# A four-layer transformer stack on one core: other order at the ends of the attentions, and transposes ahead of the first work

## The reference

```python
# L0: self-attention, cross-attention, MLP
x = x + attention(LN(x) @ w_qkv, mask=ltor) @ w_ao        # 16 heads of 16
x = x + attention(LN(x) @ w_q, enc @ w_kv, mask=cross) @ w_co
x = x + gelu_tanh(LN(x) @ w1 + b1) @ w2 + b2              # inner width 1024
# L1: RWKV block: token shift, a recurrence over 64 steps, a gated feed-forward
# L2: two cross-attentions of 16 heads of 128, then an MLP with exact gelu
# L3: cross-attention with 16 heads of 16, then an MLP with tanh gelu
```

## Time and profile before

| | us |
|---|---|
| median of 3 runs | 2081.22 |
| lowest and highest | 2080.62, 2081.76 |
| the profiled execution | 2083.29 |
| its span | 2081.5 |
| TensorE busy | 1927.9 (93%) |
| VectorE, ScalarE, GpSimd busy | 1220.0, 1049.1, 1038.6 |

### The profile page before, as it was taken

The page is one execution under the profiler, slowest core; times in us unless marked ns, Lnnn a source line. Parts: engine busy times, 40 slices in busy tenths (PEclk is TensorE's granted clock), DMA queues, the critical chain, the costliest instruction groups (busy, mean ns, idle before and its releaser), DMA issues.

```text
span 2081.5 us, 39329 instructions
## 1 busy us (share of the span) xinstructions
PE 1927.9 (93%) x15072; PEld 1567.9 (75%) x15072; DVE 1220.0 (59%) x2136; ACT 1049.1 (50%) x1949; POOL 1038.6 (50%) x1132
## 2 busy tenths in 40 slices
PE   6999799988785679999999999999999999999799
PEld 4777689433443559899989989898998988967688
DVE  3566646388999555555555555555555556745555
ACT  3665543323242356656566565656656565345542
POOL 5777731376574165445454544545444454346620
PEclk9999899989898899999999999999999999999899
DMA  4010010000000013332323332232333320010000
GB/s 183 2 42 2 2 53 1 1 0 1 1 1 31 21 44 90 90 90 86 91 79 90 89 90 90 81 95 81 90 89 88 91 67 21 21 41 2 2 11 31
DMA packets 61848, 108.08 MB, mean 52 GB/s; under 512 B 7008, under 2 KB 42336, under 8 KB 60256
## 3 DMA queue, kind: packets, MB, share of 16 engines
q1 hardware_dynamic: 60784, 103.34, 16.3%
q10 hardware_dynamic: 880, 2.22, 0.3%
HBM read 103.44 MB, written 2.10 MB: 51 GB/s over the span
## 4 chain that ended last, share of the span: by engine, by line
PE 61%; DVE 3%; issue 2%; ACT 1%; POOL 1%; DVEq 0%; ACTq 0%; POOLq 0%
PE banks L791 18%; PE banks L820 9%; PE banks L863 9%; PE banks L852 5%; PE banks L589 4%; PE banks L606 4%; PE banks L833 4%; PE banks L841 1%; PE banks L440 1%; PE banks L431 1%; PE banks L417 1%; PE banks L513 1%; PE banks L488 1%; PE banks L773 1%; ACT xn L919 1%
## 5 line engine op out<-in xcount | busy, mean ns | idle before, releaser
L1866 POOL TENSOR_TENSOR w_lo<-w2ring,w_hi 128x512 fp32r<-128x512 f32 x128 | 166.2, 1298 | 293.5 <-ACT w_hi L1187 293.5
L1246 ACT ACTIVATE PT<-banks 64x256 f32<-64x256 f32 x256 | 96.6, 377 | 264.7 <-PE banks L841 261.6
L1631 DVE SCALAR_TENSOR_TENSOR c_lo<-banks,cols,c_hi 128x512 fp32r<-128x512 f32 x128 | 96.1, 751 | 201.1 <-ACT c_hi L1211 201.1
L1875 POOL TENSOR_TENSOR wo_lo<-wo_ring,wo_hi 128x256 fp32r<-128x256 f32 x128 | 94.2, 736 | 173.3 <-ACT wo_hi L1217 173.3
L863 PE MATMUL banks<-wo_hi,c_hi 128*128 128x256 f32 x512 | 150.2, 293 | 1.8 <-POOL wo_lo L1875 1.8
L863 PE MATMUL banks<-wo_hi,c_lo 128*128 128x256 f32 x512 | 145.1, 283 | 0.0
L863 PE MATMUL banks<-wo_lo,c_hi 128*128 128x256 f32 x512 | 145.0, 283 | 0.0
L852 PEld LDWEIGHTS banks<-PT,v 128*128 128x128 f32 x1024 | 133.6, 192 | 9.0 <-ACT PT L1246 0.4
L852 PE MATMUL banks<-PT,v 128*128 128x128 f32 x1024 | 135.8, 276 | 0.3 <-ACT PT L1246 0.3
L1204 ACT ACTIVATE k<-banks,cols 128x512 f32<-128x512 f32 x128 | 88.0, 687 | 86.7 <-PE banks L791 86.7
L431 PE MATMUL banks<-xm,wl 128*128 128x512 f32 (+2 forms) x208 | 114.9, 700 | 16.1 <-DVE xm L1471 7.7
(11 more groups left out here) (219 smaller groups left out, 5773.3 us busy)
## 6 DMA issues: line engine op xcount, KB each, us to landing
w2ring<-in_w SPq DMA_DIRECT2D x128, 384.0 KB, 3.0
b2ring<-in_b SPq DMA_DIRECT2D x128, 128.0 KB, 3.3
wo_ring<-in_wo SPq DMA_DIRECT2D x128, 128.0 KB, 2.2
mlp_w<-in_mlp SPq DMA_DIRECT2D x6, 1024.0 KB, 5.4
wl<-in_wres SPq DMA_DIRECT2D x1, 2656.0 KB, 8.8
X<-in_x_in SPq DMA_DIRECT2D x4, 512.0 KB, 11.5
ctx_tok<-in_ctx_in SPq DMA_DIRECT2D x4, 512.0 KB, 16.1
wb<-in_wres SPq DMA_DIRECT2D x2, 1024.0 KB, 12.2
```

What stands on the lines that cost most here:

```text
L1246: A(PT2[keys_of, n % 2, :, r, :], held(("tp2", n))[keys_of, 0:2 * P].rearrange("p (i q) -> p i q", i=NT), ACT.Copy)\
L1631: V.scalar_tensor_tensor(c_lo[:, n % CR, :], held(("pv2", n))[:, :], col(biv, n % H2), c_hi[:, n % CR, :].bitcast(f32), ALU.add, ALU.subtr ...
L1866: G.tensor_tensor(w2_lo[:, n % 2, :], w2ring[:, n % 3, 0:2 * KT * P], w2_hi[:, n % 2, :].bitcast(f32), ALU.subtract).then_inc(S["l2_wlo"], 1)
L1875: G.tensor_tensor(wo_lo[:, n % 2, :], wo_ring[:, n % WR, :], wo_hi[:, n % 2, :].bitcast(f32), ALU.subtract).then_inc(S["l2_wolo"], 1)
```

## The change

At the start of each of the two attentions, the whole norm of the second chunk (`stats`, `roots`, `normed`) moves ahead of unit 0 on DVE, POOL and ACT; `front` stays in unit 1. At the end, the tail is written anew: ACT does its `turn` copies, exponentials and the second last `gather` before the MLP's first step; DVE does `weighed` of all units and the second last `update` before it; TensorE does `turn(29)` before the MLP's first up-product, and the rest behind its first four steps. Up-weights are split four column blocks ahead instead of two in the first and third MLP (LEAD), two of them in unit 1 and two in unit 2 of the last chunk. At the launch, TensorE waits for the identity matrix only, and transposes it 48 times (WARM) into a bank that nobody reads. `stats` gets a wait for DVE's own last aggregation.

```diff
+LEAD = (4, 2, 4)
+WARM = 48
...
@@ TensorE, attention
+                    n = UNITS * stop - 1
+                    turn(n - 2)
                     yield None
-                    for s in range(LAG + 2):
-                        if s < LAG:
-                            turn(UNITS * stop - LAG + s)
-                            weigh(UNITS * stop - LAG + s, BESIDE)
-                        if s in (0, LAG):
-                            gather(stop - 2 + (s > 0), BESIDE)
-                        if s in (1, LAG + 1):
-                            merge(stop - 2 + (s > 1), BESIDE)
-                        yield
+                    weigh(n - 2, among)
+                    gather(stop - 2, among)
+                    turn(n - 1)
+                    yield
+                    weigh(n - 1, among)
+                    turn(n)
+                    merge(stop - 2, among)
+                    weigh(n, among)
+                    yield
+                    gather(stop - 1, BESIDE)
+                    yield
+                    merge(stop - 1, BESIDE)
+                    yield
...
@@ TensorE, launch
-                pe.wait_ge(s_small, SMALL)
-                pe.wait_ge(s_once, ONCE)
+                pe.wait_ge(s_ident, 16)
+                for i in range(WARM):
+                    nc.tensor.transpose(bank[7][:, 0:P], ident, ident)
                 for k in range(KT):
                     front(0, k)
...
@@ ScalarE, attention
+                    normed(attended(start) + 1)
                     for n in range(UNITS * start, UNITS * stop):
...
-                            normed(it + 1)
+                            if ai > start:
+                                normed(it + 1)
...
-                        if p == 2 and ai + 1 == stop:
-                            for i in range(2):
+                        if p in (1, 2) and ai + 1 == stop:
+                            for i in range(2 * p - 2, 2 * p):
                                 up_weights_hi(a0, i)
                         yield 1
-                    exp(UNITS * stop - 2)
+                    n = UNITS * stop - 1
+                    turn(n - 2)
+                    exp(n - 1)
+                    gather(stop - 2)
+                    turn(n - 1)
+                    exp(n)
+                    turn(n)
                     yield None
-                    for s in range(LAG + 1):
-                        if s == 0:
-                            exp(UNITS * stop - 1)
-                        if s < LAG:
-                            turn(UNITS * stop - LAG + s)
-                        if s in (0, LAG):
-                            gather(stop - 2 + (s > 0))
-                        yield
+                    yield
+                    yield
+                    gather(stop - 1)
+                    yield
...
@@ ScalarE, mlp (GpSimd's likewise)
-                        if n + 2 < MT:
-                            up_weights_hi(m, n + 2)
+                        if n + LEAD[m] < MT:
+                            up_weights_hi(m, n + LEAD[m])
...
@@ VectorE, stats and attention
+                    if it:
+                        dve.wait_ge(S["ln_mv"], NT * it)
...
+                    stats(attended(start) + 1)
                     dve.wait_ge(S["vbd_preset"], 1 if a0 == 0 else 2)
...
-                    largest(UNITS * stop - 1)
-                    weighed(UNITS * stop - LAG - 1)
+                    n = UNITS * stop - 1
+                    largest(n)
+                    for i in range(LAG):
+                        weighed(n - LAG + i)
+                    update(attended(stop - 2))
+                    weighed(n)
                     yield None
...
@@ GpSimd, attention
+                    roots(attended(start) + 1)
                     for n in range(UNITS * start, UNITS * stop):
...
-                        if p == 0:
+                        if p == 0 and ai > start:
                             roots(attended(ai) + 1)
```

More of the change, by code:

```diff
@@ L308, in build @@
             sem, ("vectors_in", "w_qkv_in", "w_self_in", "w_cross_in", "w_l1_in", "w_l3_in", "preset", "masks_in", "rows_in", "state_in"))
-        s_rows0, s_sel = sem("first_rows_in"), sem("select_in")
+        s_ident, s_rows0, s_sel = sem("ident_in"), sem("first_rows_in"), sem("select_in")
         s_x = [sem(f"x_in{c}") for c in range(CHUNKS)]
@@ L401, in build @@
         NS = KT * S8
-        SMALL, ONCE = 5 * 16, 1
+        SMALL, ONCE = 4 * 16, 1
         with nc.Block() as block:
@@ L1014, in mlp @@
                     if m == 1:
-                        for i in range(2):
+                        for i in range(LEAD[m]):
                             up_weights_hi(m, i)
@@ L1396, in attention @@
                             values(ai + 1, 0)
-                        if n == UNITS * start:
-                            stats(it + 1)
-                        else:
+                        if n > UNITS * start:
                             largest(n - 1)
@@ L1411, in attention @@
                         yield 1
-                    largest(UNITS * stop - 1)
-                    weighed(UNITS * stop - LAG - 1)
-                    yield None
-                    for s in range(LAG + 2):
-                        if s < LAG:
-                            weighed(UNITS * stop - LAG + s)
-                        if s in (1, LAG + 1):
-                            update(attended(stop - 2 + (s > 1)))
-                        yield
+                    n = UNITS * stop - 1
[4 more added lines that the diff above has]
+                    weighed(n)
+                    yield None
+                    yield
+                    yield
+                    yield
+                    update(attended(stop - 1))
+                    yield
                 def mlp(m):
@@ L1672, in _ @@
                 stats(0)
-                dve.wait_ge(s_small, SMALL)
                 dve.wait_ge(s_rows0, 16)
@@ L1760, in mlp @@
                         it = first + c
-                        if n + 2 < MT:
-                            up_weights_lo(m, n + 2)
+                        if n + LEAD[m] < MT:
+                            up_weights_lo(m, n + LEAD[m])
                         if c == 0:
@@ L1953, in _ @@
                 chunk_in(X, 0, t_x, s_x[0])
-                sp.dma_start(consts[:, 0:P], t_consts[:, 0:P]).then_inc(s_small, 16)
+                sp.dma_start(consts[:, 0:P], t_consts[:, 0:P]).then_inc(s_ident, 16)
                 load_weights(sp, s_w0, wa, "L0_qkv", "L0_ao")
```

## The result

| | before | after |
|---|---|---|
| median, both kernels in turn on one chip | 2081.49 (4 runs, 2080.62 to 2083.73) | 2048.76 (4 runs, 2048.59 to 2049.86) |
| ratio, 95% interval | | 0.9842 (0.9825 to 0.9859) |
| span of the profiled execution | 2081.5 | 2048.0 |

A forecast was written before the change was run, and what follows sets the result against it. TensorE bounds nearly all stages, so edits pay only where it idles or runs at the lower clock. Gains of 7.3 (attention 0's start), 3.3 (attention 2's start) and 19.0 (both joins) sum to 29.6: 2051.6, range 2041 to 2065.

The forecast's parts named there:

- Rival 1: Launch: the clock ignores the warm-up transposes, costing 6.1 + 0.6 us, total 2058; chance 0.12.
- The term 3.7 + 3.4: Attention 0's first chunk: TensorE's 3.7 us wait for xn goes, and 3.4 us of low clock behind it.
- the gain is carried on: From 50 to 240 us TensorE is nearly always busy, so the start's 7.3 us gain is kept.
- 28.0: Each join, from `turn(28)` to the sixth up-product: TensorE's own work, unchanged, 28.0 us.
- (a): Each join, ahead of `weigh(28)`: the first wait stays and grows by some 0.6, to 3.1 us.
- (b): Each join, from `turn(29)` to `turn(31)`: at most 0.8 us of waits.
- (c): Each join: a new 3.2 us wait of `merge(7)`, behind statistics, roots, xn and the copies of `gather(7)`.
- (d): Each join: low clock from `weigh(28)` on, perhaps again after the later wait, 3.3 us in all.
- Rival 2: The joins bring only 6 us each, through a longer `merge(7)` wait and clock fall; 2059 to 2066, chance 0.18.
- 0 to 0.5: The recurrence, 390 to 700 us: cost of DVE's new wait in `stats`, 0 to 0.5 us.
- Rival 3: No clock fall in joins, 13 us each; low stretch after 1877.24 gone, 4.7; 2039 to 2046, chance 0.17.
- Rivals 4 and 5: Clock stays low into feed-forward chunks, 2092, chance 0.04; recurrence takes gains back, within 4 us of 2081, chance 0.04.

The follow-up runs named there:

- e4: The changed kernel with no warm-up transposes (WARM = 0), only the shorter launch wait; median 2050.46, ratio 0.9849.
- e5: The changed kernel with POOL's 2.34 us bias addition of the second chunk two units later, in each attention's first chunk; median 2046.77, ratio 0.9839.
- e1: The kernel before with only the second chunk's norm moved ahead of unit 0, in both attentions; median 2072.69, ratio 0.9953.
- e6: The changed kernel with the norm of the first and third MLP's second chunk moved to the attention's end; median 2036.03, ratio 0.9792.
- e9: The changed kernel with LEAD = (2, 2, 2), two up-weight column blocks split in unit 2 alone; median 2051.06, ratio 0.9860.
- e3: The kernel before with only the new attention tail and LEAD, without the launch and second-chunk norm edits; median 2059.33, ratio 0.9894.
- e10: The changed kernel with the late bias, the early norm for the MLP's second chunk, and 32 warm-up transposes for 48; median 2030.24, ratio 0.9760.
- e2: The kernel before with only the launch edit: wait for the identity alone, 48 transposes, no DVE wait for small inputs; median 2079.12, ratio 0.9989.
- e12: The kernel before with only the ring of four single banks moved on by three at the start of attention 2; median 2075.05, ratio 0.9975.

## Why the prediction was right, and where it was not

**The warm-up: right.** Forecast: 48 transposes from 6.0, their end between 14.5 and 15.4, net +0.6. Measured: 6.15 to 13.8, and +0.5 on average over the profiles (+0.83 against e4 alone). The end came sooner because one of a row of transposes takes 0.21 and 0.11 us; the forecast's 0.24 and 0.13 were eighths of rows of eight, with the last one's whole length in them. Rival 1, the clock that ignores transposes, is out. Windows of after that hold nothing on TensorE but these transposes, with their count in the first bracket:

```profile
6.00:8.00 2.00, 1.85 (x9) 1.00 0.95 388
10.00:12.00 2.00, 2.00 (x18) 1.00 1.02 371
```

9 in the busy 1.85 us are 0.21 us each, 18 in 2 us are 0.11. The granted clock is printed as 1.00 in both; at the launch the durations tell, not that column. By the rule in the Trainium skill, "TensorE: Matmul & The Clock Gate", Part 4, this rise should not come from transposes; here it did.

**Chunk 1's norm in attention 0: the step that failed.** The term 3.7 + 3.4 was right up to `turn(0)` (7.76 in all for 7.3). What failed is "POOL's chain of masks and `lowered` [...] ends `lowered(0)` near 34.9, before TensorE's first `turn`", taken as the end of the matter, and behind it "the gain is carried on". The first half is true (34.3), but I followed one product, T of unit 0, and not the queue of its next consumer. `weigh(0)` needs PT(0)'s copy, which stands on ACT behind `exp(1)`, and that waits for five POOL instructions without a gap. Before the change `turn(0)` ended at 45.6, and `exp(1)` had started at 43.20: TensorE met none of it. The busy 184 of 190 us in 50 to 240 were no proof either: the loss is at its edge, from 41.3 to 53.6. The term and the warm-up together are 3.0 with the give-back; e5 shows that a 2.34 us addition that nobody needed yet costs 3 to 4.

**Attention 2's start: right**, 3.75 for 3.3 (e1: 3.76). In after, `front(33)` at 1827.72 waits for nothing.

**The joins: right in kind, one term mis-sized.** Forecast, from `turn(28)` to the sixth up-product: 28.0 + (a) 3.1 + (b) 0.8 + (c) 3.2 + (d) 3.3 = 38.4. Measured 39.62: (a) 2.93, (b) 0, (c) 3.94. The low clock is read row by row: `weigh(28)` 0.25 (1.38 for 1.13), `turn(29)` 0.88, `merge(7)` 3.07, 4.2 in all. Taken for every row, against the shortest that it is in seven profiles with this order, it is 4.6, and 28.1 of work is left. Join 2 took 38.95, with the same waits and 3.5 of low clock. Term (d) is thus 4.6 and 3.5 for 3.3, (c) 3.94 for 3.2, and (b) 0 for 0.8: I gave the fall behind (c) almost nothing, and `merge(7)` then ran 6.69 for 3.62. The work and (a) were good. Before, the same stretch had 13.55 idle and 6.1 of low clock, so of the 8.2 gained in join 1, 6.7 are idle time and 1.5 are clock. (c) was on the right chain, statistics, roots, norm, copies of `gather(7)`, and e6 confirms it: without (c) and its fall each join gains 6.0 and 6.5 more. Rival 2, joins of 6 only, had the same mechanism with a higher price and came to 2059; the measured 8.2 and 8.8 lie nearer to the forecast. e9 shows that four blocks for two, which (a) charged with 0.6, lengthen the first wait by 1.4.

**The recurrence: outside the forecast.** I had 0 to 0.5 and profiles differ here by up to 5, before against before by 2.35. It is no gain that I can put down to the change. The prediction's own sign, "I am wrong if the warm-up runs at 0.24 us throughout, or if the stretches from 50 to 240 or from 390 to 1735 change their lengths by over 2 us", came true in it. What it is worth in the medians isn't settled: the parts that are shown sum to 3.0 + 8.2 + 3.75 + 4.3 + 8.85 + 0.3 = 28.4, the medians differ by 32.7. The same sum leaves -1.3 (e3) to 3.4 (e6) in the other kernels with an edit. The other 4.3 fits no edit, and e4, e5, e9 and e10 with their medians 30 to 51 us below before have the same 3 to 5 in their profiles, as have e1, e2 and e12. Which moments of the clock's fall make the stage long or short was not tried.

**The third chunk of attention 2: right size, wrong reason, in a rival.** Rival 3 let the low stretch behind the 2.07 us wait go "by another phase", 4.7. It went, 4.3, but by the banks, as e12 shows. e12 came to `scores(35)` 4.57 us earlier too, but that is not it: e2 came 5.9 and e1 9.6 us earlier, and both have the wait of 2.08 and its low stretch still, while e12 has the two sets of four with 1.64 idle ahead of the second, just as after and e3, whose shifts there are 20.0 and 12.8. The forecast says nothing of `among`; it names not only a place to put results but a counter that the next attention inherits.

**Rivals 4 and 5** did not come: behind the joins the feed-forward keeps its length (81.9 us from the sixth up-product to the recurrence before, 81.7 in after), and nothing was given back in the recurrence.

**The sum.** That 2048.76 lies 2.8 from the forecast of 2051.6 is in part luck: 6.3 us too much in three terms stand against 9.4 us of which the sum had nothing.

## What to carry to other kernels

When a stall is removed, follow not the awaited tile alone but the queue of the next consumer on each engine for the next few units: work that the stall had hidden (here a bias that nobody needed, worth 3 to 4 us) becomes the new wait, and moving it costs one line. Price a wait on TensorE with the low clock that follows it: here 3.94 us idle cost 6 to 7 in all. And where banks are taken from a running counter, an edit in one stage changes which buffers collide in another; compare stages that were not edited too.

## What the hardware showed that I had not expected

A train of transposes alone brings TensorE's clock up: 9 in the first 2 us, 18 in the third stretch of 2 us. How long it takes differs between executions: the same 48 transposes took 7.1 to 8.3 us in six profiles. Two waits differ in what follows: 2.07 us in one piece, up to 1877.24, was followed by eight transposes in 1.97 us, 1.64 us between two sets of four (after, as e12) by a stretch at 1.00; whether the length or the split decides can't be told from these two. A stage that no edit touches, the recurrence, differs by 5 us of 383 between profiled executions, with equal busy times of DVE, ACT and POOL and different clocks of TensorE.
